# A fused SSM-convolution and FFN kernel: shorter table chain, channel 0 in halves, convolution pieces one slot ahead

## The reference

```python
dtA = (-exp(log_A_real) + 1j * A_imag) * exp(log_dt)[:, None]
Ct = C * (exp(dtA) - 1.0) / A
K = 2.0 * einsum('hn,hnl->hl', Ct, exp(dtA[:, :, None] * arange(L))).real   # taps, per channel
y = (causal convolution of u with K) + u * D[:, None]
y = y * (arange(L) < length)
hidden = silu(q(y) @ gate.T) * (q(y) @ up.T)                                # q: rounding to fp8
out = x + q(hidden) @ down.T
```

## Time and profile before

| | before |
|---|---|
| median of 3 runs | 326.05 us (325.91 to 326.08) |
| profiled run | 326.16 us |
| its span | 324.4 us |
| granted clock, mean | 1.00 |
| PE busy | 310.2 us, 96% |
| DVE busy | 303.4 us, 94% |
| ACT busy | 206.3 us, 64% |

### The profile page before, as it was taken

One profiled execution on the slowest core, in us unless ns is written; L12 is line 12 of the kernel. 1 busy time (PEld: TensorE's weight loads), 2 busy tenths in 40 slices (PEclk: granted clock), 3 DMA queues, 4 the chain that ended last, 5 costly groups with the idle time before them and its releaser, 6 DMA issues.

```text
span 324.4 us, 4763 instructions
## 1 busy us (share of the span) xinstructions
PE 310.2 (96%) x1567; PEld 162.7 (50%) x1593; DVE 303.4 (94%) x464; ACT 206.3 (64%) x318; POOL 12.5 (4%) x20
## 2 busy tenths in 40 slices
PE   1999899999999999999999999999999999989996
PEld 1557554545455554555455544555455454534444
DVE  6989999999999999999998999989998999989784
ACT  4839788278755777476844868366863959364540
POOL 2031000000001000010001000010001000010010
PEclk9999999999999999999999999999999999999999
DMA  5779999400001690077302780067401650051028
GB/s 203 169 179 226 259 277 379 174 1 0 2 0 17 131 359 15 1 129 266 122 0 26 154 337 1 0 116 249 154 0 16 132 242 1 0 100 31 0 34 226
DMA packets 14014, 38.38 MB, mean 118 GB/s; under 512 B 1470, under 2 KB 6558, under 8 KB 11052
## 3 DMA queue, kind: packets, MB, share of 16 engines
q1 hardware_dynamic: 8412, 26.58, 23.1%
q0 software_dynamic: 5584, 11.57, 20.5%
HBM read 33.90 MB, written 15.81 MB: 153 GB/s over the span
## 4 chain that ended last, share of the span: by engine, by line
PE 75%; DVE 16%; issue 4%; ACT 3%; DMA 2%; DVEq 0%; ACTq 0%; SPq 0%
PE gate_ps L535 19%; PE up_ps L535 18%; PE down_ps L491 17%; PE y_ps L477 16%; DVE hv L834 3%; DVE yq L818 3%; DVE yt L807 2%; DVE hq L851 2%; DVE ht L842 2%; PE y_ps L576 1%; DVE ym L799 1%; PE down_ps L576 1%; DMA toep<-kpad_scratch 1%; PE gate_ps L456 1%; PE y_ps L459 1%
## 5 line engine op out<-in xcount | busy, mean ns | idle before, releaser
L392 ACT ACTIVATE sil<-gate_ps,fac 128x512 f32<-128x512 f32 (+1 forms) x88 | 59.7, 680 | 67.8 <-PE gate_ps L535 66.8
L535 PE MATMUL gate_ps<-yq,wg 128*128 128x512 bf16 (+3 forms) x365 | 88.1, 362 | 2.7 <-DVE hv L834 2.4
L535 PE MATMUL up_ps<-yq,wu 128*128 128x512 bf16 (+3 forms) x367 | 88.4, 363 | 0.3
L477 PE MATMUL y_ps<-xt,toep 128*128 128x512 f32 (+3 forms) x256 | 80.4, 434 | 0.5 <-DMA toep<-kpad_scratch 0.5
L491 PE MATMUL down_ps<-wd,hq 128*128 128x512 bf16 (+1 forms) x295 | 76.8, 379 | 0.8
L834 DVE SCALAR_TENSOR_TENSOR hv<-up_ps,fac,sil 128x512 f32<-128x512 f32 (+1 forms) x88 | 65.6, 745 | 8.2 <-ACT sil L392 6.6
L375 ACT ACTIVATE hc<-hv 128x1024 f32<-128x1024 f32 (+1 forms) x48 | 47.1, 980 | 20.9 <-DVE hq L851 19.8
L477 PEld LDWEIGHTS y_ps<-xt,toep 128*128 128x128 f32 x256 | 47.2, 190 | 21.4 <-issue 2.9
L535 PEld LDWEIGHTS gate_ps<-yq,wg 128*128 128x128 bf16 x372 | 35.6, 100 | 43.7 <-ACT sil L392 4.0
L842 DVE SCALAR_TENSOR_TENSOR ht<-hc,hv 128x1024 f32<-128x1024 f32 (+1 forms) x48 | 54.2, 1129 | 1.9 <-ACT hc L375 1.8
L535 PEld LDWEIGHTS up_ps<-yq,wu 128*128 128x128 bf16 x372 | 36.3, 100 | 38.3
(11 more groups left out here) (149 smaller groups left out, 113.0 us busy)
## 6 DMA issues: line engine op xcount, KB each, us to landing
xt<-in_xT SPq DMA_DIRECT2D x8, 1024.0 KB, 7.6
out<-in_x SPq DMA_DIRECT2D x7, 1024.0 KB, 5.7
out<-res POOLq DMA_DIRECT2D x7, 1024.0 KB, 7.8
toep<-kpad_scratch SPq DMA_DIRECT2D x6, 1024.0 KB, 9.8
toep<-kpad_scratch SPq DMA_DIRECT2D x8, 256.0 KB, 4.3
wd<-in_down POOLq DMA_DIRECT2D x1, 1280.0 KB, 21.6
xt<-in_x SPq DMA_DIRECT2D x1, 1024.0 KB, 7.2
out<-xt SPq DMA_DIRECT2D x3, 256.0 KB, 3.1
```

Source lines behind the costliest of these rows:

```text
L392: nc.scalar.activation(sil[b][0:w, :], gate_ps[b][0:w, :], ACT.Silu, scale=fac[0:w, S_GATE:S_GATE + 1]).then_inc(silu_done, 1)
L477: last = nc.tensor.matmul(y_ps[h % 2][:, d * P:L], toep[par][:, h, d * P:(d + 1) * P], xt[par][:, h, 0:L - d * P], start=(d == 0), stop=(d ...
L535: mm = nc.tensor.matmul(ps[b][0:w, cols], wt[:, k, c * P:c * P + w], yq[par][:, version, k, cols], start=(k == 0), stop=(k == LB - 1))
```

## The change

1. WARM[0] is 2 instead of 3.
2. In DVE's chain, `s(15)` and `s(16)` are made by one operation, `less` and `expx` go (their work is put into `scalar_tensor_tensor` operations), and the decay product of group 0 (`decayed(0)`, before the first operation of `g_of(0)`) stands ahead of the last steps of the chain.
3. The taps of group 0 are copied by DVE, behind the second operation on the turns of group 1; `copy_k(2)` on ACT stands ahead of channel 3 instead of behind it.
4. Channel 0 of block 0 is convolved in two halves of 256 columns, in two PSUM banks; DVE masks each half, ACT scales the first and DVE the second.
5. `CONV_PLAN` has each piece one slot earlier; the piece of distance 0 of channel 2 of block 1 goes between the third and the fourth channel's products of block 0. `mask_y(g + 2, 0)` goes from slot 10 to slot 9, `sum_y` of channel 3 from slot 8 to slot 9, behind the product of that slot.
6. SP issues the loads for block 3 ahead of the copy of x for block 0.

```diff
-WARM = (3, 14)
+WARM = (2, 14)
...
+        def first_bank(half):
+            return up_ps[0] if half else y_ps[0]
...
-                sp.wait_ge(k_copied, 2 * (b + 1))
+                if b:
+                    sp.wait_ge(k_copied, 2 * b)
+                else:
+                    sp.wait_ge(k_first, 2)
...
+            next_conv(3, 1)
             copy_x(0, 0)
-            next_conv(3, 1)
             copy_x(1, 1)
...
             nc.scalar.activation(sil[0][:, 0:1], fac[:, 0:1], ACT.Silu)
-            copy_k(0)
             waves(1)
...
             for h in range(HB):
+                if h == HB - 1:
+                    copy_k(2)
                 if h:
                     scale_y(0, h)
                 else:
+                    cols = slice(0, L // 2)
+                    act.wait_ge(ym_first, 1)
+                    nc.scalar.activation(yv[0][:, 0, cols], ym[0][:, cols], ACT.Copy,
+                                         scale=fac[:, D_GATE:D_GATE + 1]).then_inc(yv_first, 1)
+                    nc.scalar.activation(yv[0][:, 1, cols], ym[0][:, cols], ACT.Copy,
+                                         scale=fac[:, D_UP:D_UP + 1]).then_inc(yv_first, 1)
                     act.wait_ge(ym_done, 1)
                 magnitude_y(0, h)
-            copy_k(2)
...
                 for step, h, distances in CONV_PLAN.get(c, ()):
-                    if step <= ahead and (down or (step, h) != (1, 1)):
+                    if step <= ahead and (down or c):
...
-            for h in range(HB):
+            pe.wait_ge(toep_first[0], 16)
+            pe.wait_ge(xt_in[0], 16)
+            for half, hi in enumerate((L // 2, L)):
+                lo = half * L // 2
+                for d in range(hi // P):
+                    out_lo = max(lo, d * P)
+                    last = nc.tensor.matmul(first_bank(half)[:, out_lo:hi], toep[0][:, 0, d * P:(d + 1) * P],
+                                            xt[0][:, 0, out_lo - d * P:hi - d * P], start=(d == 0),
+                                            stop=(d == hi // P - 1))
+                last.then_inc(y_ready if half else y_first, 1)
+            for h in range(1, HB):
                 conv(0, 0, 0, h, [0, 1, 3, 2])
...
             by_channel(2)
+            conv(1, 1, 0, 2, [0])
             by_channel(3)
...
-            a = did(v.tensor_tensor(s(15), ai, dt, ALU.mult))
-            v.tensor_tensor(s(16), ai, dt, ALU.mult)
+            a = did(v.tensor_tensor(s(15, 2), both(ai), both(dt), ALU.mult))
...
-            v.tensor_scalar(less, two_x, -1.0, None, ALU.add)
...
-            b = did(v.tensor_tensor(expm1, qx, less, ALU.add))
+            b = did(v.scalar_tensor_tensor(expm1, two_x, -1.0, qx, ALU.add, ALU.add))
...
-            b = did(v.tensor_scalar(expx, expm1, 1.0, None, ALU.add))
...
-            a = did(v.tensor_tensor(sr, sr, expx, ALU.mult))
-            b = did(v.tensor_tensor(si, s(SIN), expx, ALU.mult))
+            a = did(v.scalar_tensor_tensor(sr, expm1, 1.0, sr, ALU.add, ALU.mult))
+            b = did(v.scalar_tensor_tensor(si, expm1, 1.0, s(SIN), ALU.add, ALU.mult))
+            damped = [decayed(0)]
...
             w = did(v.tensor_scalar(whole[:, js], turns[:, js], MAGIC, MAGIC, ALU.add, ALU.subtract))
+            for half in range(2):
+                dve.wait_ge(k_ready, half + 1)
+                v.tensor_copy(rows_of_k(0, half), k_in_bank(0, half)).then_inc(k_first, 1)
...
+                    if ahead == 2 and c == 9:
+                        mask_y(g + 2, 0)
                     if c == CH - 1:
-                        if ahead == 2:
-                            mask_y(g + 2, 0)
...
-            mask_y(0, 0)
-            dve.wait_ge(ym_done, 1)
-            v.tensor_scalar(yv[0][:, 0, :], ym[0][:], f(D_GATE), None, ALU.mult)
-            link(v.tensor_scalar(yv[0][:, 1, :], ym[0][:], f(D_UP), None, ALU.mult))
+            for half, computed in enumerate((y_first, y_ready)):
+                cols = slice(half * L // 2, (half + 1) * L // 2)
+                dve.wait_ge(computed, 1)
+                masked = v.tensor_tensor(ym[0][:, cols], first_bank(half)[:, cols],
+                                         mask[:].rearrange("p k b -> p (k b)")[:, cols], ALU.mult)
+                if half:
+                    masked.then_inc(ym_done, 1)
+                    dve.wait_ge(ym_done, 1)
+                    v.tensor_scalar(yv[0][:, 0, cols], ym[0][:, cols], f(D_GATE), None, ALU.mult)
+                    link(v.tensor_scalar(yv[0][:, 1, cols], ym[0][:, cols], f(D_UP), None, ALU.mult))
+                else:
+                    masked.then_inc(ym_first, 1)
...
 CONV_PLAN = {
-    7: [(2, 0, [0])], 8: [(2, 0, [1, 3])], 9: [(2, 0, [2]), (2, 1, [0])], 10: [(2, 1, [1, 3])],
-    0: [(1, 1, [2])], 1: [(1, 2, [0])], 2: [(1, 2, [1, 3])], 3: [(1, 2, [2]), (1, 3, [0])],
-    4: [(1, 3, [1, 3])], 5: [(1, 3, [2])],
+    6: [(2, 0, [0])], 7: [(2, 0, [1, 3])], 8: [(2, 0, [2]), (2, 1, [0])], 9: [(2, 1, [1, 3])], 10: [(2, 1, [2])],
+    0: [(1, 2, [0])], 1: [(1, 2, [1, 3])], 2: [(1, 2, [2]), (1, 3, [0])], 3: [(1, 3, [1, 3])], 4: [(1, 3, [2])],
 }
...
-SUM_PLAN = {2: 0, 3: 1, 6: 2, 8: 3}
+SUM_PLAN = {2: 0, 3: 1, 6: 2, 9: 3}
```

More of the change, by code:

```diff
@@ L168, in adaln_ffn_kernel @@
         k_ready, k_copied = sem("k_ready"), sem("k_copied")
+        k_first = sem("k_first")
         gate_ready, up_ready, silu_done = sem("gate_ready"), sem("up_ready"), sem("silu_done")
@@ L173, in adaln_ffn_kernel @@
         y_ready, ym_done, yscaled = sem("y_ready"), sem("ym_done"), sem("yscaled")
-        yc_first = sem("yc_first")
+        yc_first, y_first, ym_first, yv_first = sem("yc_first"), sem("y_first"), sem("ym_first"), sem("yv_first")
         yt_done, yr_done, yq_ready = sem("yt_done"), sem("yr_done"), sem("yq_ready")
@@ L540, in slots @@
                         beside(g, par, half, c, down, ahead)
-            for h in range(HB):
+            pe.wait_ge(toep_first[0], 16)
[9 more added lines that the diff above has]
+            for h in range(1, HB):
                 conv(0, 0, 0, h, [0, 1, 3, 2])
             k_of(2)
-            pe.wait_ge(k_copied, 4)
+            pe.wait_ge(k_copied, 2)
             pe.wait_ge(up_in, 16)
@@ L554, in _ @@
             slots(0, 0, 0, False, 2)
-            pe.wait_ge(k_copied, 2 * len(K_GROUPS))
+            pe.wait_ge(k_copied, 2 * (len(K_GROUPS) - 1))
             pe.wait_ge(down_in, 32)
@@ L614, in _ @@
             thetas, kt, r = s(15, 3), s(0, 3), s(10, 3)
-            x, kx, rx, qx, two_x, less = s(19), s(20), s(21), s(22), s(23), s(24)
-            expm1, expx, norm, half = s(25), s(26), s(27), s(28)
+            x, kx, rx, qx, two_x = s(19), s(20), s(21), s(22), s(23)
+            expm1, norm, half = s(25), s(27), s(28)
             c_ai, c_ar, g = s(29, 2), s(31, 2), s(33, 2)
@@ L680, in steps, with decayed @@
                 return table.broadcast_to([P, js.stop - js.start, 3, KA])
+            def decayed(i):
+                js = K_GROUPS[i]
+                n = js.stop - js.start
+                dve.wait_ge(wave_ready, i + 1)
+                dve.wait_ge(dec_ready, FIRST if i == 0 else FIRST + 2)
+                return did(v.tensor_tensor(wave[:, js], wave[:, js],
+                                           dec[:, js].rearrange("p j (t m) -> p j t m", t=1).broadcast_to([P, n, 2, M]),
+                                           ALU.mult))
             after(a)
@@ L730, in _ @@
             after(c)
-            b = did(v.tensor_tensor(expm1, qx, less, ALU.add))
+            b = did(v.scalar_tensor_tensor(expm1, two_x, -1.0, qx, ALU.add, ALU.add))
             dve.wait_ge(sines_ready, 1)
             a = did(v.scalar_tensor_tensor(sr, s(SIN_HALF), -2.0, s(SIN_HALF), ALU.mult, ALU.mult))
-            after(b)
-            b = did(v.tensor_scalar(expx, expm1, 1.0, None, ALU.add))
             c = did(v.tensor_tensor(g, g, both(norm), ALU.mult))
-            after(b)
-            a = did(v.tensor_tensor(sr, sr, expx, ALU.mult))
-            b = did(v.tensor_tensor(si, s(SIN), expx, ALU.mult))
+            after(a)
+            a = did(v.scalar_tensor_tensor(sr, expm1, 1.0, sr, ALU.add, ALU.mult))
+            b = did(v.scalar_tensor_tensor(si, expm1, 1.0, s(SIN), ALU.add, ALU.mult))
+            damped = [decayed(0)]
             after(a)
@@ L756, in g_of @@
                 js = K_GROUPS[i]
-                n = js.stop - js.start
-                dve.wait_ge(wave_ready, i + 1)
-                dve.wait_ge(dec_ready, FIRST if i == 0 else FIRST + 2)
+                w = damped[0] if i == 0 else decayed(i)
                 after(a)
-                w = did(v.tensor_tensor(wave[:, js], wave[:, js],
-                                        dec[:, js].rearrange("p j (t m) -> p j t m", t=1).broadcast_to([P, n, 2, M]),
-                                        ALU.mult))
                 after(w)
@@ L920, in sum_half @@
             def sum_half(part):
+                dve.wait_ge(yv_first, part + 1)
```

## The result

The changed kernel takes **334.73 us** (median of 4 runs, 333.67 to 335.13), the kernel before 326.06 us beside it (325.91 to 326.28): a ratio of 1.0258 [1.0245, 1.027]. It is 8.7 us slower; the forecast was 3.8 us slower, with 327.9 to 330.8 as its range. The profiled run took 334.80 us, with a span of 333.1 where before had 324.4.

A forecast was written before the change was run, and what follows sets the result against it. PE's work sets the end, plus DVE's lateness in blocks 0 to 1 and 6 to 7. Terms 3.06 + 0.2 + 0.55 = 3.8 us on the 326.05 us median gave 329.8 us, range 327.9 to 330.8.

The forecast's parts named there:

- Head: Start of the kernel: shorter table chain and DVE's tap copies let the first convolution start 0.41 us earlier.
- rival 4: Warm-up: PE's clock rises later, the first convolution starts 1.7 us late, 331.5 us in all; chance 0.08.
- Block 0 to 1: DVE's sum (0.12 us) and mask (0.60) cost time; a 2 us wait replaces the 0.60; nothing gained in front.
- The slot ahead: Block 2, slot 6: toep lands at 124.2, PE stops for 2.9 us, block 3 starts 3.06 us later.
- the piece starts at 124.2 as before: Block 2: the piece reading toep starts unchanged with a slot more behind it, 3.02 us.
- From then on the store follows PE's block, so this is paid once: After block 2: the toep stall does not recur, except 0.2 us added for block 5.
- Block 6 to 7: Fuller slot 0 makes gate_ready 0.43 us later, sum and round add 0.12: 0.55 us at PE's end.
- The sign looked for: Block 7: PE's wait grows to about 2 us.
- Rivals 2 and 3: Block 2: no toep stall, 326.6 us (chance 0.10); or also y chain's 0.8 us reaching block 1, 325.2 (0.05).
- rival 2: Block 2: toep's load is in time, no stall; 0.1 in front and 0.55 or less remain: 326.6 us; chance 0.10.
- The estimate from it, 4.4 us for 1 MB: Toep's load by the skill's DMA fit: landing at 118.6, no stall, 326.7 us; the trace's 9.9 us was preferred.

The follow-up runs named there:

- head_only: The kernel before with points 1 to 4 of the change alone, plans and SP's order as before; 325.57 us, ratio 0.9978.
- sum_back: The changed kernel with y's last sum back in slot 8, ahead of the tenth product; 331.66 us, ratio 1.0146.
- lf_res: loads_first with the convolution piece (1, 3, [2]) given out in slot 5 again and slot 4 left empty; 327.17 us, ratio 1.0029.
- half_ahead: Kernel before with the change's head, loads ahead of the store's wait, only pieces for the block after next a slot earlier, slot 0 without convolution; 325.39 us.
- loads_first: The changed kernel with SP's loads of xt and toep issued ahead of the store's wait and the copy of x; 328.20 us, ratio 1.0053.
- copy_last: The changed kernel with the copy of x behind the loads of xt and toep, both still behind the store's landing; 328.19 us, ratio 1.0055.

## Why the prediction was off

The sign, the place of the largest wait and its release were right. By the prediction's steps:

**Head.** The table chain and DVE's copies came as laid out, and toep landed at 17.53 (forecast 17.57). The convolution started at 18.02, so the 0.41 us didn't arrive in this run. What held it is PE itself, in its timeline of after:

```profile
12.50 4.87 PE L460 MATMUL y_ps<-wg 128*128 128x512 bf16 x14
17.30 0.64 PE L451 MATMUL gate_ps<-res,hq 64*16 64x32 f32 x32
18.02 0.92 PE L561 MATMUL y_ps<-xt,toep 128*128 128x256 f32 x4
```

The clock rose later than in the earlier trace rows, and about eight of the fourteen matmuls were slow (8 x 0.43 and 6 x 0.22 us are 4.8). This is rival 4's mechanism at about a quarter of its price (18.02 less 17.57, of 1.7). The step that failed is that the head's gain was taken as whole: `head_only` realised 0.33 us of it, after none. With the same head other traces have the start at 17.69 to 18.04, so how much arrives varies from run to run.

**Block 0 to 1.** Confirmed. DVE's timeline of after around the tenth product, beside the earlier trace rows:

```profile
60.02 0.74 DVE L862 SCALAR_TENSOR_TENSOR hv<-up_ps,fac,sil 128x512 f32<-128x512 f32 x1
60.69 1.22 DVE L835 SCALAR_TENSOR_TENSOR yt<-yc,yv 128x1024 f32<-128x1024 f32 x1
...
63.54 0.68 DVE L827 TENSOR_TENSOR ym<-y_ps,mask 128x512 f32<-128x512 f32 x1
...
67.19 1.23 DVE L870 SCALAR_TENSOR_TENSOR ht<-hc,hv 128x1024 f32<-128x1024 f32 x1 [0.72 <-ACT hc L381]
```

The wait for ym was 1.96 us (forecast 2), the idle time ahead of the sum at 67.19 was 0.72 (forecast 0.85). From 60.02 on everything was about 0.5 us later than forecast, which is the head's missing 0.41; that and 0.23 for ACT's result are most of the +0.89 at which block 2 starts.

**The slot ahead.** Toep was issued at 114.32 (about 114.2 forecast) and landed at 124.19 (124.2). The chain of store, copy and load was followed rightly to a tenth. PE stopped for 2.2 us by the starts of its matmuls and not 2.9: it came 1.0 us later itself (0.76 at the start of the block, 0.23 by the hole), and the piece started 0.2 us after the landing, at 124.42. The sum ("the piece starts at 124.2 as before") is indifferent to the first. What was missing is behind the wait: the clock at half for 3.4 us, 1.7 us. The prediction had TensorE's lower level in its reach, in rival 4, and looked for it in the head alone.

**"From then on the store follows PE's block, so this is paid once"** is the step that failed with the largest size, 2.1 us in block 5. The store does follow the block, but 1.06 us later in it than before, because the sum stands behind a product that waits for PE. I had costed the sum's new place only where DVE has no idle time (0.12 us), and took idle time on DVE as cover. It isn't one for work that stands behind the wait. The terms of block 5: 0.2 as forecast, 1.18 for the later issue (12.08 us into the block against 10.90), 0.74 for a load of 11.64 us instead of 10.9, less 0.23 because the hole lets PE come later itself: 1.9, and PE's wait is 1.92. `sum_back` showed the first two: store at +1.61, wait 0.94.

**Not in the prediction at all:** with nothing in slot 5, PE gets to the second bank of down 0.43 us sooner and waits 0.23 us for ACT, six times, 1.4 us. `lf_res` showed it; by its span 1.0 to 1.2 us of that is time, as block 6's hole costs nothing. I had moved each piece forward and asked for each what it needs itself; I hadn't asked what the slot left empty had covered.

**Block 6 to 7.** 0.57 us against 0.55, and `half_ahead` confirms the mechanism with the other sign. `sum_back` splits the 0.57: 0.44 stays with the sum back in slot 8, and 0.13 is the sum, where 0.43 and 0.12 were forecast. The 0.12 doesn't carry over: in `half_ahead` the same move cost 0.73 us. The sign looked for, a wait of about 2 us in block 7, came otherwise: PE waits 0.61 us for ACT's result and then 1.22 for the product, where before it waited 1.17 for the product alone (all by the starts of its matmuls).

**Rivals 2 and 3** (the load in time) didn't come about, but `loads_first` and `copy_last` are what rival 2 would be. It was priced at 326.6 and they take 328.2: the small holes of blocks 1 to 5 (1.15 us) are most of the difference, and what is missing of the head's gain (0.15 us in the trace of `loads_first`, 0.47 in that of `copy_last`) is a part of the rest.

The Trainium skill (DMA: Bandwidth & Descriptors, section Anatomy of one DMA) gives its fit for DMAs that GpSimd issues; these are issued by SP, which the prediction did not say. The estimate from it, 4.4 us for 1 MB, is below each of the loads of toep: 7.2 to 8.4 us in `loads_first`, with only xt ahead, 8.0 to 8.2 with the copy behind, 9.6 to 11.6 behind the copy. The load of xt, issued first in `copy_last`, comes near it with 4.8.

By terms, the 4.9 us between forecast and result are: front 0.8, the hole of block 1 in it; in block 2 the clock 1.7 and the 0.2 from landing to piece, less 0.8 because the block started later and the wait was shorter by that; in blocks 3 and 4 the holes for ACT 0.5 and small waits of 0.1 us around the loads 0.4; in block 5 2.1, the wait being 1.7 of it.

## What to carry to other kernels

When work is moved a slot ahead, ask three things of it: what its inputs' chain has in hand (a load 1.1 us in hand can't be asked for 3 us sooner), what the slot that becomes empty was covering, and what now stands behind a waiting instruction on its engine. Idle time ahead of an instruction covers what stands before the wait and nothing that stands behind it. Issue a load when its buffer is free, ahead of bulk copies and of waits that concern others: by itself it gave nothing here, but it made the plan's largest cost go, and it costs one moved line.
